# The first three rounds of a perceiver layer with another order of work: Hadamard mean in round 0, ternary compares over rounds 1 and 2

## The reference

```
cq = layernorm(x) @ Wq_d;  ckv = ctx @ Wkv_d            # 64 and 32 latent columns
s  = (cq @ W_qk) by head @ ckv.T / sqrt(32);  a = softmax(s)      # 16 heads
x  = x + (a @ (ckv @ Wv_u) by head)
q, k, v = layernorm(x) @ Wqkv + bqkv                    # one head of 128
x  = x + softmax(q @ k.T / sqrt(128)) @ v @ Wo + bo
h  = layernorm(x) @ hadamard                            # 512 x 512
hq = clip(round(h / step), -8, 7) * step,  step = max|h| / 7 of a row
w  = ternary(weight) * scale,  scale = mean|weight| of a row
x  = x + hq @ w.T
```

## Time and profile before

| what | us |
|---|---|
| median of 3 runs (lowest, highest) | 325.86 (325.75, 326.93) |
| the profiled execution's own time | 325.88 |
| its span | 324.1 |
| PE busy in the span | 309.0 |
| DVE busy | 239.9 |
| ACT busy | 211.5 |
| POOL busy | 88.7 |

### The profile page before, as it was taken

How to read it: one execution, slowest core, us unless ns; L and a number is a source line. 1 busy time by engine, 2 the same in 40 slices (tenths; PEclk the granted TensorE clock), 3 DMA queues, 4 the chain that set the end, 5 groups by cost and what they waited for, 6 DMA issues and landing times.

```text
span 324.1 us, 8470 instructions
## 1 busy us (share of the span) xinstructions
PE 309.0 (95%) x3157; PEld 218.6 (67%) x3172; DVE 239.9 (74%) x517; ACT 211.5 (65%) x581; POOL 88.7 (27%) x129
## 2 busy tenths in 40 slices
PE   8987999999999999999999999999999999999995
PEld 6765766767576867667576857666675767575754
DVE  1599458886888678886879678886888778886335
ACT  1485877767585777767686877766776868682310
POOL 2000634140323224240333224240414123232220
PEclk9999999999999999999999999999999999999999
DMA  7992402050301403050302302050302010000000
GB/s 219 292 385 66 146 3 97 2 188 10 129 3 50 148 3 128 0 193 1 129 0 93 101 32 97 0 194 0 129 2 69 0 67 1 34 3 32 0 34 32
DMA packets 13482, 25.25 MB, mean 78 GB/s; under 512 B 3217, under 2 KB 3985, under 8 KB 13457
## 3 DMA queue, kind: packets, MB, share of 16 engines
q1 hardware_dynamic: 13456, 24.91, 23.0%
HBM read 20.71 MB, written 4.19 MB: 77 GB/s over the span
## 4 chain that ended last, share of the span: by engine, by line
PE 66%; DVE 18%; ACT 5%; issue 3%; DMA 3%; SPq 2%; POOL 1%; DVEq 0%; POOLq 0%
PE ps L684 14%; PE ps L722 6%; PE ps L632 6%; PE ps L799 5%; PE ps L831 4%; PE ps L642 4%; PE ps L822 4%; DVE sum_a L459 4%; PE ps L779 3%; PE ps L726 3%; DMA w_rows<-weight 3%; DVE mx L450 3%; PE ps L734 2%; PE ps L649 2%; PE ps L805 2%
## 5 line engine op out<-in xcount | busy, mean ns | idle before, releaser
L320 ACT ACTIVATE prob<-ps,nmx,qk_scale 128x128 f32<-128x128 f32 x256 | 96.1, 466 | 41.3 <-DVE nmx L454 41.3
L684 PE MATMUL ps<-had_s,x3t 128*128 128x512 f32 x128 | 59.2, 605 | 2.9 <-ACT x3t L314 2.7
L450 DVE TENSOR_REDUCE mx<-ps 128x8 f32<-128x1024 f32 x32 | 39.0, 1218 | 16.3 <-PE ps L799 16.3
L684 PEld LDWEIGHTS ps<-had_s,x3t 128*128 128x128 f32 x128 | 23.0, 189 | 32.3 <-issue 28.4
L459 DVE TENSOR_REDUCE sum_a<-prob 128x8 f32<-128x1024 f32 x32 | 37.5, 1210 | 2.4 <-ACT prob L320 2.4
L303 POOL TENSOR_TENSOR qk_scale<-aux,power 128x1 f32<-128x1 f32 x16 | 8.8, 550 | 98.6 <-DVE aux L534 98.6
L314 ACT ACTIVATE prob_t<-ps 128x512 f32<-128x512 f32 x64 | 35.2, 622 | 0.5
L632 PE MATMUL ps<-ident,prob 128*128 128x128 f32 x256 | 33.7, 275 | 0.6 <-ACT prob L320 0.6
L307 POOL TENSOR_TENSOR res<-prod,x 128x512 f32<-128x512 f32 x15 | 19.1, 1277 | 54.4 <-DVE prod L567 54.4
L722 PE MATMUL ps<-x2t,wqkv_s 128*128 128x128 f32 x256 | 32.6, 281 | 0.4 <-ACT x2t L314 0.4
L722 PEld LDWEIGHTS ps<-x2t,wqkv_s 128*128 128x128 f32 x256 | 29.8, 191 | 1.9 <-ACT x2t L314 1.0
(11 more groups left out here) (119 smaller groups left out, 543.7 us busy)
## 6 DMA issues: line engine op xcount, KB each, us to landing
ct<-ctx_cols SPq DMA_DIRECT2D x16, 512.0 KB, 4.7
xt<-x_cols SPq DMA_DIRECT2D x16, 256.0 KB, 2.7
xr<-x_rows SPq DMA_DIRECT2D x16, 256.0 KB, 4.2
y<-res SPq DMA_DIRECT2D x15, 256.0 KB, 2.0
w_rows<-weight SPq DMA_DIRECT2D x1, 1024.0 KB, 8.3
had_s<-hadamard SPq DMA_DIRECT2D x1, 1024.0 KB, 8.4
wqkv_s<-wqkv SPq DMA_DIRECT2D x1, 768.0 KB, 10.0
wqk<-w_qk SPq DMA_DIRECT2D x2, 128.0 KB, 4.4
```

The lines of the kernel that those rows point to most:

```text
L320: last = nc.scalar.activation(prob[:, h, :], ps[:, h // 4, (h % 4) * P:(h % 4) * P + P], ACT.Exp, bias=nmx[:, h:h + 1], scale=qk_scale[:])
L450: V.tensor_reduce(mx[:, h], ps[:, 2 * half:2 * half + 2, :].rearrange("p r (c k) -> p (r c) k", c=EC), AX.X, ALU.max).then_inc(done["mx"], 1)
L684: mm = pe.matmul(ps[:, B4, :], x3t[:, c, :], had_s[:, c, :], start=(c == 0), stop=(c == EC - 1))
```

## The change

- **SP**: `had_s` is loaded where `w_rows` was; `w_rows` and `wqkv_s` are loaded after the queries and the context of pair 2.
- **PE, round 0**: the projection of pair 1 comes before the transposes of prob, between 4 and 8 filler matmuls (12 where there were 14). The Hadamard mean is made in pieces of 2, 1 and 1 matmuls between the transposes, the scores and the weighted sum. The scores of pair 1 come before the weighted sum. No ternary transposes are left here.
- **PE, round 1**: paired projection, turning of x2 and second half of the transposes of prob stand ahead of L722; `wide_scale` and the transposes of the first two ternary row blocks stand near its end. **Round 2**: the transposes of the other two, between v and the second half of prob's transposes.
- **DVE**: takes three copies of round 0 from ACT (q_t, ckv, one of four prob_t); both maxima of pair 1 stand at the end of round 0; sums, row statistics and scales are put in another place; w_abs is four instructions (two in round 0, two in round 1); ternary row blocks 0 and 1 (one w_neg and one tern each) stand in round 1, to either side of the second maximum, row blocks 2 and 3 in round 2 ahead of the statistics of x3.
- **ACT**: the copies follow these orders; `tern_t` is copied by half in rounds 1 and 2. **POOL**: qk_scale stands before the Hadamard subtractions.

The diff, cut to its core (what moves without other change on ACT is left out):

```diff
             sp.dma_start(bo_row[:], bo.rearrange("(o n) -> o n", o=1).to_broadcast([P, E])).then_inc(ld_w["b"], 16)
-            sp.dma_start(w_rows[:], weight.rearrange("(c p) n -> p c n", p=P)).then_inc(ld_w["w"], 16)
+            sp.dma_start(had_s[:], hadamard.rearrange("(c p) n -> p c n", p=P)).then_inc(ld_w["had"], 16)
             sp.dma_start(wo_s[:], wo).then_inc(ld_w["wo"], 16)
             sp.wait_ge(zero_wv, 1)
             for r in range(4):
                 sp.dma_start(wv_bd[32 * r:32 * r + 32, :, 32 * r:32 * r + 32],
                              wv_u.rearrange("l (c r d) -> l c r d", c=EC, r=4)[:, :, r, :]).then_inc(ld_w["wv"], 16)
             load_rows(1, 1)
-            sp.dma_start(had_s[:], hadamard.rearrange("(c p) n -> p c n", p=P)).then_inc(ld_w["had"], 16)
-            sp.dma_start(wqkv_s[:], wqkv.rearrange("(c p) n -> p c n", p=P)).then_inc(ld_w["wqkv"], 16)
             sp.wait_ge(made["lat"], 1)
             load_queries(2, 0)
             load_context(2, 0)
+            sp.dma_start(w_rows[:], weight.rearrange("(c p) n -> p c n", p=P)).then_inc(ld_w["w"], 16)
+            sp.dma_start(wqkv_s[:], wqkv.rearrange("(c p) n -> p c n", p=P)).then_inc(ld_w["wqkv"], 16)
...
-                if isinstance(i, int) and i == 1:
-                    hadamard_centred()
                 if front:
                     after(pool, done["aux1"], i + 1)
                     nc.gpsimd.tensor_tensor(qk_scale[:], aux1[:], power[:], ALU.pow).then_inc(done["qk_scale"], 1)
+                if isinstance(i, int) and i == 1:
+                    hadamard_centred()
...
+                def ternary_copy(half, bank):
+                    act.wait_ge(ternt_made, half + 1)
+                    copy(tern_t[:, :, 2 * half * P:2 * (half + 1) * P],
+                         ps[:, bank, :].bitcast(BF16).rearrange("p (c o) -> p c o", c=EC)).then_inc(ternt_read, 1)
+
...
-            def ternary():
+            def weight_sizes(c0, c1):
                 dve.wait_ge(ld_w["w"], 16)
-                V.tensor_reduce(w_abs[:], w_rows[:], AX.X, ALU.add, apply_absolute_value=True).then_inc(wabs_done, 1)
-                dve.wait_ge(wabs_done, 1)
+                for c in range(c0, c1):
+                    V.tensor_reduce(w_abs[:, c:c + 1], w_rows[:, c, :], AX.X, ALU.add, apply_absolute_value=True)\
+                        .then_inc(wabs_done, 1)
+
+            def weight_scales():
...
+            def output_bias():
+                dve.wait_ge(cb_made, 1)
+                V.tensor_tensor(const_row[:], ps[:, B4, :], bo_row[:], ALU.add).then_inc(const_ready, 1)
+
+            def ternary(c):
                 dve.wait_ge(whalf_done, 1)
-                for c in range(EC):
-                    if c:
-                        dve.wait_ge(tern_done, c)
-                    V.tensor_scalar(w_neg[:], w_rows[:, c, :], w_nhalf[:, c:c + 1], None, ALU.is_lt).then_inc(neg_done, 1)
-                    dve.wait_ge(neg_done, c + 1)
-                    V.scalar_tensor_tensor(tern[:, c, :], w_rows[:, c, :], w_half[:, c:c + 1], w_neg[:], ALU.is_gt,
-                                           ALU.subtract).then_inc(tern_done, 1)
+                if c:
+                    dve.wait_ge(tern_done, c)
+                V.tensor_scalar(w_neg[:], w_rows[:, c, :], w_nhalf[:, c:c + 1], None, ALU.is_lt).then_inc(neg_done, 1)
+                dve.wait_ge(neg_done, c + 1)
+                V.scalar_tensor_tensor(tern[:, c, :], w_rows[:, c, :], w_half[:, c:c + 1], w_neg[:], ALU.is_gt,
+                                       ALU.subtract).then_inc(tern_done, 1)
...
-                if cross:
+                if cross and not (first and i == 1):
                     largest(i, 1)
-                if isinstance(i, int) and i == 0:
+                if first and i == 0:
                     dve.wait_ge(ld_w["b"], 64)
                     V.tensor_copy(bv_wide[:], b_qkv[:, 2:3].to_broadcast([P, P])).then_inc(bvw_done, 1)
-                    ternary()
-                    dve.wait_ge(cb_made, 1)
-                    V.tensor_tensor(const_row[:], ps[:, B4, :], bo_row[:], ALU.add).then_inc(const_ready, 1)
+                    dve.wait_ge(made["qt"], 2)
+                    V.tensor_copy(q_t[:, 1], ps[:, B2, :].rearrange("p (c b q) -> p b c q", c=EC, b=2)).then_inc(read["qt"], 1)
+                    dve.wait_ge(made["ckv"], 2)
+                    V.tensor_copy(ckv[:, 1], ps[:, B1, 0:2 * SKV]).then_inc(read["ckv"], 1)
+                    sums(0)
+                    dve.wait_ge(made["pt"], 1)
+                    V.tensor_copy(prob_t[:, 0, :, :], ps[:, 0, :].rearrange("p (c t) -> p c t", c=EC)).then_inc(read["pt"], 1)
+                    row_variance()
+                    dve.wait_ge(done["exp"], 2)
+                    row_scale()
+                    sums(1)
+                    weight_sizes(0, 2)
+                    dve.wait_ge(made["s"], 2)
+                    largest(1, 0)
+                    largest(1, 1)
+                if first and i == 1:
+                    output_bias()
+                    weight_sizes(2, EC)
+                    weight_scales()
+                    dve.wait_ge(done["rsum"], 1)
+                    sums(0)
+                    sums(1)
+                    row_variance()
+                    row_scale()
+                    ternary(0)
+                    second_max()
+                    ternary(1)
+                if first and i == 2:
+                    ternary(2)
+                    ternary(3)
...
-                if cross:
+                if cross and not (first and i <= 1):
...
+                if self_ and not (first and i == 1):
+                    second_max()
...
+                if front and not (first and 0 <= i <= 1):
+                    row_variance()
+                    row_scale()
...
-                if front:
+                if front and not (first and i == 0):
...
                 pe.wait_ge(wide_done, 1)
-                pe.wait_ge(hmean_read, 1)
+                pe.wait_ge(const_ready, 1)
...
+            def hadamard_mean(c0, c1):
                 pe.wait_ge(ld_w["had"], 16)
-                pe.wait_ge(ternt_read, 1)
+                for c in range(c0, c1):
+                    mm = pe.matmul(ps[:, B3, :], mean_w[:], had_s[:, c, :], start=(c == 0), stop=(c == EC - 1))
+                if c1 == EC:
+                    mm.then_inc(hmean_made, 1)
+
+            def ternary_transposed(half, bank):
+                pe.wait_ge(tern_done, 2 * (half + 1))
                 for c in range(EC):
...
+                    for o in range(2):
+                        col = (2 * c + o) * P
                         mm = pe.transpose(ps[:, bank, :].bitcast(BF16)[:, col:col + P],
-                                          tern[:, o, (2 * half + c) * P:(2 * half + c + 1) * P], ident_b[:])
+                                          tern[:, 2 * half + o, c * P:(c + 1) * P], ident_b[:])
...
+                    if first and i == 2:
+                        pe.wait_ge(ternt_read, 1)
...
-                if first and i == 1:
-                    hadamard_mean()
...
+                if self_ and not (first and i == 1):
+                    x2_turned()
                 if cross:
                     if first and i == 0:
-                        keep_busy(10, B3)
+                        keep_busy(4, B4)
+                        after(pe, read["lat"], i + 1)
+                        projected()
+                        keep_busy(8, B4)
                     transposed(0)
                     transposed(1)
                 if first and i == 0:
-                    after(pe, read["lat"], i + 1)
-                    projected()
+                    hadamard_mean(0, 2)
                     wide_bias()
+                if first and i == 1:
+                    paired_projection()
+                    x2_turned()
+                    transposed(2)
+                    transposed(3)
                 if self_:
                     if first and i == PAIRS:
                         keep_busy(2, 0)
...
+                if front and par == 1 and not alone(i) and not (first and i == 1):
+                    paired_projection()
+                if first and i == 2:
+                    pe.wait_ge(read["pt"], i * 4 + 1)
+                    ternary_transposed(1, 0)
+                if cross and not (first and i == 1):
                     transposed(2)
                     transposed(3)
...
                 if first and i == 0:
-                    keep_busy(4, B3)
-                if first and i == 1:
-                    wide_scale()
+                    hadamard_mean(2, 3)
...
                     if first and i == 1:
-                        pe.wait_ge(ternt_read, 2)
+                        pe.wait_ge(hmean_read, 1)
...
-                if cross:
+                def weighted_sum():
...
+                    if first and i == 2:
+                        pe.wait_ge(ternt_read, 2)
...
+
+                if first and i == 0:
+                    scores()
```

(16 more changed lines are left out.)

144 lines of the change are left out of this document (74 added, 70 removed).

## The result

The changed kernel takes **325.58 us** (median of 20 runs, 324.11 to 327.64), and the kernel before, timed in turn with it on one chip, 326.27 us (20 runs, 325.59 to 328.82). The ratio is 0.9967 [0.9952, 0.9983]: 0.3% faster, with the whole interval under 1 (the medians alone give 0.2%). That is inside the half per cent that I had counted as no change, and on the other side of it from the forecast of 327.0 us, 0.3% slower. The profiled executions took 325.41 and 325.88 us, with spans of 323.6 and 324.1 us.

A forecast was written before the change was run, and what follows sets the result against it. PE was busy 309.0 of 324.1 us, with DVE 0.27 us from bounding round 2. xm 1.25 us earlier, less 2.62 for compares, plus 0.24 of slack, made 1.1 us later: 325.88 + 1.1 = 327.0 us, range 325.0 to 328.9.

The forecast's parts named there:

- Round 0 on PE: PE, round 0: waits and two fillers go, the Hadamard mean (3.5 us) comes; L642 of round 1 0.75 us sooner.
- w_rows and the maxima: Load queue and DVE, round 0: w_rows lands at 22.8 or up to 1 us later, maxima of pair 1 at 24.7.
- Rival 4: Round 0: w_rows lands at 25 or later, so the maxima come late; 1 us more, 328.0 us; chance 0.05.
- Round 1 on PE: PE, round 1: Hadamard mean leaves, a 1.55 us wait comes before the paired projection; L642 of round 2 2.85 us earlier.
- My 0.55 for the late row statistics: DVE, round 1: pair 2's row statistics delay the second maximum; its scores lose 0.55 us, leaving 2.3 of 2.85.
- The hold by GpSimd: Round 1: DVE's ternary instructions and nmx wait for POOL's Hadamard subtractions; xm at 46.8, 1.25 us earlier instead of 2.3.
- Round 2: DVE, round 2: two compares add 2.62 us before the statistics of x3; scores of pair 3 1.1 us later than before.
- From the scores of pair 3 on the order is the old one, so the shift stays to the end: Everything behind the scores of pair 3: the 1.1 us delay stays unchanged to the end, giving 327.0 us.
- nothing is held: Round 1: ternary instructions pass beside POOL, xm 2.3 us earlier; 325.9 us, or 325.4 with xr early; chance 0.28.
- POOL keeps its turn: Round 1: DVE gets in only after all four POOL subtractions, xm 0.5 us later than before; 328.8 us; chance 0.2.
- The third: Round 2: DVE has slack and is not the bound, so PE's shift alone counts; 323.4 us; chance 0.07.

The follow-up runs named there:

- e1: The changed kernel with GpSimd's Hadamard subtractions waiting until both ternary rows of round 1 are made; 326.71 us, 0.9998 of the kernel before.
- e2: The changed kernel without the compares of ternary rows 2 and 3, those blocks filled with ones; 325.06 us, 0.9959 of the kernel before.
- e5: The kernel before with seven one-column memsets on VectorE ahead of the loop; 325.70 us, 0.9984 of the kernel before.

## Why the prediction was wrong

Step by step, with the start (0.43) taken off the times of the changed kernel. Each step is one trace against one, so at pair 3 the landing of `w_rows` (0.9 us between four traces) stands behind these tenths:

- **Round 0 on PE: right.** L642 of round 1 was forecast at 27.05; measured 26.99.
- **w_rows and the maxima: right.** Forecast landed at 22.8 and up to 1 us later, measured 22.8 by VectorE's wait; the maxima of pair 1 start at 24.4, forecast 24.7. Rival 4 (25 or later) fell.
- **Round 1 on PE: right within 0.3.** The wait before the paired projection is 1.51 us, forecast 1.55; L642 of round 2 at 44.41, forecast 44.1. My 0.55 for the late row statistics was taken off xm behind this: the second maximum came at 38.71 (forecast 38.8), and its cost shows as the 0.27 us before the transpose of p2. It is inside the 44.41, so that 2.55 us reached xm where the forecast had 2.3 before the hold: 0.25 of the error.
- **The hold by GpSimd: right in kind, wrong in size and in what it means for the path. This is the failed step.** I wrote that row 0 waits some 0.5 us for qk_scale, that each of the two instructions of row 1 waits for one subtraction of 1.24 us, that nmx of pair 2 waits to 45.6, and "x3 and xm stand behind nmx. xm then starts at 46.8". Measured (start left in): nothing lost on row 0 (0.48 and 0.75; it was qk_scale that grew, from 0.55 to 0.72), 0.69 and 0.89 us lost on w_neg and tern (1.17 and 1.64 against 0.48 and 0.75), and 0.74 on nmx (0.97 against 0.23), which ends at 44.71, 0.03 behind the subtractions. Without the start GpSimd began them at 38.39, where I had taken 39.4 out of my 38.6 to 39.4, and they took 5.86 us instead of some 6.2, so nmx ended at 44.28 instead of 45.6. And there x3 waited not for nmx but for PE's L925 (the wait of 0.34 in VectorE's timeline): **xm came at 45.50**, right behind L709. I had let the hold take 1.05 of 2.3 us, and it took none. e1 shows it from the other side: 3.93 us with row 1 not held, 3.92 with it held. This is 1.05 of the 2.2 us by which the sum was off, and with the 0.25 above it is the whole 1.3 at xm (46.8 against 45.50).
- **Round 2: right in what bounds it, nearly right in size.** Forecast 2.62 us between xm and the statistics of x3 for the two compares, measured 2.56 (6.75 against 4.19); from xm to the scores of pair 3 2.24 more than before, forecast 2.38. PE waits for 0.84 us before the transpose of p2 and 0.89 before L751, and e2 shows that without the compares 1.09 of the round comes back. The rest, some 1.1 us of PE and ACT work, is hidden while VectorE is last, as the forecast had it; it would have cost that and not the 0.45 that I gave it. (The 0.03 us for a semaphore in that sum stands in no row.) Round 2 accounts for 0.14 of the error.
- **"From the scores of pair 3 on the order is the old one, so the shift stays to the end": wrong.** The order is the old one, the time isn't: 0.75 us, which e5 gives back to the kernel before with seven memsets. No row that I read spoke of it, though the gap of 0.46 us in round 4 stood in the trace. This is the rest.

Together 1.05 + 0.25 + 0.14 + 0.75 = 2.2 us, which is the way from +1.1 to -1.06. In the medians the change is worth -0.7 us, by the ratio of runs timed in turn -1.1; in the profiled pair -0.47, the 0.43 of a later start being in it.

Of the rivals, the first (*nothing is held*, 325.9 or 325.4) came nearest in time and is false as a mechanism: both instructions of row 1 are held. Its time came out near by luck, from a hold that cost nothing and a loop gain that no rival had. The second (*POOL keeps its turn*) fell: w_neg gets in after one subtraction. The third fell as well, since PE waits in round 2. What the list lacked is the case "held, but behind nothing that is late": I summed the delay along VectorE's own order and didn't set it against what PE hands over meanwhile. Two hand-overs covered it. The maxima of pair 2 need the scores, which ended at 42.12 (in e1, with row 1 not held, VectorE stands idle for them), and tern ended at 42.32. And x3 needs L925, right ahead of L709 in PE's order, so my own 44.1 for the one gave the other; nmx had 0.33 us of room there, which with my 45.6 would not have been enough. The size and the missing comparison failed together.
